# Sending the negated row maxima in two halves, and a new written order of a fused audio tower's attention step

## The chip, the cores and the metric

The kernel runs on one core of one Trainium2 chip. The metric is the device time of one execution in microseconds (us). All times below are of that kind, or are starts and durations of single instructions in one profiled execution, counted from its first instruction.

## The reference

The input is x of 16 sequences (batches) by 256 frames by 128 features. What is computed, cut to what matters:

```python
h = batchnorm(relu(window5(x) @ W.T + b))              # (16, 252, 256)
xn = layernorm(h)
q, k, v = (xn @ Wq, xn @ Wk, xn @ Wv)                  # 16 heads of 16
sim = q @ k.T * 16 ** -0.5 + bias[head, i - j]         # causal: -inf where j > i
h = h + softmax(sim) @ v @ Wo + bo
h = h + ffn(layernorm(h))        # quantised: scales from maxima over the whole tensor
```

## The kernel before, in words

The program has three parts: loading and splitting of weights (to about 64 us), the attention part over 16 batches (to about 496 us), and the feed-forward part, which needs a maximum over all batches and so begins when the last batch is through.

A sequence has N = 252 rows, cut into two tiles of TT = 126. Matrix products run on pairs of f16 values (a high and a low part: `qh`/`ql`, `kh`/`kl`, `xnh`/`xnl`, `onh`/`onl`), accumulated in PSUM. The softmax takes two passes over the scores. Pass P1 puts scores with rows on the partitions into PSUM (line 648 for the bias, line 651 for the product), and VectorE takes the row maxima of each piece (line 803) into `mx`. The maxima of all 16 heads are then turned by TensorE (`mT`, line 659), negated by ScalarE into `mneg` (line 918) and sent by a DMA of the SP queue (line 990) into row 65 of the stacked q tile `q_st`, where the keys' stack holds a row of ones. Pass P2 (line 669) computes the transposed scores with the maximum already subtracted, VectorE adds the bias (line 794, `sbr`), ScalarE takes the exponential (line 879, `pt`), and `PV` multiplies with v (lines 684 and 688). Each pass has 12 pieces a batch: pieces 0 to 5 hold heads 0 to 7, pieces 6 to 11 heads 8 to 15. Each piece uses one of four PSUM banks in turn, and may be written once VectorE has read the piece four places before.

The batches are pipelined through a step b of a loop: P2 and PV of batch b, q, k, v and P1 of batch b+1, the convolution of b+2, the load and transposition of x of b+3, and the second layer norm (`h2`, `stats2`, `xn2`, `x2T`, `x2`) of batch b-1, with the maximum `ax` of batch b-2. Steps -2 to 1 and 12 to 16 are written out, steps 2 to 11 are a loop of two steps a turn. Within a step each engine runs a list written out by hand: `PE_ORDER`, `DVE_ORDER`, `ACT_ORDER` (lines 449 to 462). An entry is a stage and the offset of its batch. An engine runs its list strictly in that order, and each stage waits for the semaphores of its inputs and of the buffers it overwrites.

Stages that need a PSUM bank for a short time share two, listed in `MISC` (lines 496 to 498): bank 6 goes to `q`, `conv`, `xnT` in turn, bank 7 to `mT`, `k`, `x2T`, `v`, `xT`, `OT0`, `onT`. `misc_free` (line 509) makes a stage on TensorE wait until the reader of the stage ahead of it in the ring is done. So before the change `k` waits for `mneg_r`, the sign that `mneg` has read `mT`'s result, and `conv` waits for `ql_r`, the sign that `ql` has read that of `q`.

Around the turn of a step, the orders before are:

```
PE : ... P1[9] P1[10] xnT P1[11] wo | mT q k P2[0..3] conv0 P2[4] conv1 x2T P2[5] conv2 P2[6] PV0 conv3 P2[7] ...
DVE: ... P1[9] onl P1[10] P1[11] xnl | h2 stats2 ql kl ax P2[0] ... P2[11] P1[0] ...
ACT: ... xn onh xnh | mneg qh kh xn2 P2[0..2] x2 P2[3..6] osb0 P2[7..9] relu P2[10] P2[11] osb1 va ...
```

`h2` adds the attention's output to the residual (line 855), `stats2` takes its mean and variance (lines 819, 824), GpSimd turns these into a scale and a shift (lines 952 to 958), ScalarE applies them (`xn2`, line 913), TensorE turns the result (`x2T`, line 726), ScalarE copies it out (`x2`, line 944) and VectorE takes its largest value (`ax`, line 860). `relu` (line 902) begins the chain of the first layer norm over GpSimd (lines 966 to 975), `va` (line 935) copies v out of bank 7. SP's list (`sp_step`, line 985) is: the DMA of `mneg`, six DMAs of q and k into their stacks, the load of x, the store of the residual.

Of the kernel before, what the change touches and what calls it, by code (L numbers as in the profile page):

```python
# [26 lines left out]
ACT = mybir.ActivationFunctionType  # L27
# [5 lines left out]
N = T - CTX + 1  # L33
TT = N // 2
# [37 lines left out]
def audio_tower(nc, x, cw, cb, gamma, beta, rmean, rvar, wq, wk, wv, wo, bo, rel, wg, wu, wd, hot, eyes, out):  # L72
    with ExitStack() as ctx:
# [77 lines left out]
        kS = [sba(f"k_st{i}", [128, H, NP], F16) for i in range(2)]  # L151
        va = [sba(f"va{i}", [128, 2, H, 32]) for i in range(2)]
        qh, ql, kh, kl = (sba(n, [128, 2, NP], F16) for n in ("qh", "ql", "kh", "kl"))
        mneg = sba("mneg", [H, NP], F16)
        qks = sba("qks", [128, 2])
        wam = sba("wam", [128, 8])
        wal = sba("wal", [128, 8])
# [197 lines left out]
        def dve_first(dve):  # L355
            nc.vector.memset(nhalf[:], -0.5).then_inc(S["nhalf_set"], 1)
            nc.vector.memset(epsc[:], EPS).then_inc(S["nhalf_set"], 1)
            nc.vector.memset(minus[:], -1.0).then_inc(S["nhalf_set"], 1)
            nc.vector.memset(lt_s[:, 0:TT - 1], MASKED).then_inc(S["lines_sb"], 1)
            nc.vector.memset(ln_s[:, N:LINE], MASKED).then_inc(S["lines_sb"], 1)  # L360
            for t in kS:
                nc.vector.memset(t[:].rearrange("p h n -> p (h n)").bitcast(F32), TWO_ONES
                                 ).then_inc(S["dve_init"], 1)
            for t in (qh, ql, kh, kl):
                nc.vector.memset(t[:, :, N:NP], 0.0).then_inc(S["dve_init"], 1)
            nc.vector.memset(mneg[:, N:NP], 0.0).then_inc(S["dve_init"], 1)
            dve.wait_ge(S["lines_ps"], 2)
            nc.vector.tensor_copy(lt_s[:, TT - 1:LINE], ps[0:H, 0, TT - 1:LINE]).then_inc(S["lines_sb"], 1)
            nc.vector.tensor_copy(ln_s[:, 0:N], ps[0:H, 1, 0:N]).then_inc(S["lines_sb"], 1)
            dve.wait_ge(S["cw_in"], 16)  # L370
            nc.vector.tensor_reduce(wam[:, 0:1], cw_n.rearrange("p a b -> p (a b)"), X, ALU.max,
                                    apply_absolute_value=True).then_inc(S["wamax"], 1)
            dve_step(dve, -3, 1)
            power(dve, 0, 1, 1, 4, 256)
            dve.wait_ge(S["winv_s"], 1)
            for j in range(len(banks)):
                lo_of(dve, j)
            dve.wait_ge(S["w_loaded"], 64)
# [12 lines left out]
            nc.vector.tensor_tensor(bc[:, 2, :], bc[:, 2, :], shift, ALU.subtract).then_inc(S["vec_ready"], 1)
            dve.wait_ge(S["anti_in"], 16)
            nc.vector.tensor_copy(antib[0:TT], anti[0:TT]).then_inc(S["dve_init"], 1)
            power(dve, 1, 5, 2, 5, 0)
            dve.wait_ge(S["winv_s"], 2)
            nc.vector.tensor_scalar(qks[:, 0:1], wscale[:, W_Q:W_Q + 1], DH ** -0.5, None, ALU.mult
                                    ).then_inc(S["dve_init"], 1)
            nc.vector.tensor_copy(qks[:, 1:2], wscale[:, W_K:W_K + 1]).then_inc(S["dve_init"], 1)
            for t in va:
                nc.vector.memset(t[:, :, :, DH:32], 1.0).then_inc(S["dve_init"], 1)  # L400
            lo_of(dve, len(banks))
            lo_of(dve, len(banks) + 1)
# [46 lines left out]
        PE_ORDER = [("mT", 0, 0), ("q", 1, 0), ("q", 1, 1), ("k", 1, 0), ("k", 1, 1)] + P2[0:4] + [
                    ("conv", 2, 0), P2[4], ("conv", 2, 1), ("x2T", -1, 0), P2[5], ("conv", 2, 2), P2[6], ("PV", 0, 0),  # L450
                    ("conv", 2, 3), P2[7], ("conv", 2, 4), P2[8], ("conv", 2, 5), P2[9], ("PV", 0, 1), P2[10], P2[11],
                    ("v", 1, 0), P1[0], ("v", 1, 1), P1[1], ("PV", 0, 2), P1[2], P1[3], ("xT", 3, 0), P1[4],
                    ("PV", 0, 3), P1[5], P1[6], ("OT0", 0, 0), ("OT1", 0, 0), P1[7], P1[8], ("onT", 0, 0), P1[9],
                    P1[10], ("xnT", 2, 0), P1[11], ("wo", 0, 0), ("wo", 0, 1)]
        DVE_ORDER = [("h2", -1), ("stats2", -1), ("ql", 1), ("kl", 1), ("ax", -2)] + P2 + P1[0:4] + [
                     ("stats", 2), P1[4], ("xl", 3), P1[5], ("on", 0, 0), P1[6], ("on", 0, 1), P1[7], P1[8], P1[9],
                     ("onl", 0), P1[10], P1[11], ("xnl", 2)]
        ACT_ORDER = [("mneg", 0), ("qh", 1), ("kh", 1), ("xn2", -1)] + P2[0:3] + [("x2", -1)] + P2[3:7] + [
                     ("osb", 0, 0)] + P2[7:10] + [("relu", 2)] + P2[10:12] + [
                     ("osb", 0, 1), ("va", 1), ("osb", 0, 2), ("xh", 3), ("osb", 0, 3), ("xn", 2), ("onh", 0),  # L460
                     ("xnh", 2)]


        FF_BANKS = len(ff_banks)
# [17 lines left out]
        def step_order(engine, b):  # L482
# [6 lines left out]
            for st in order:  # L489
                if runs(b, st[1]):  # L490
# [2 lines left out]

        MISC = [[("q", "ql_r", 1, 1, 1), ("conv", "relu_r", 1, 1, 2), ("xnT", "xnl_r", 1, 1, 2)],
                [("mT", "mneg_r", 1, 1, 0), ("k", "kl_r", 1, 1, 1), ("x2T", "x2_r", 1, 1, -1), ("v", "va_r", 1, 1, 1),
                 ("xT", "xl_r", 1, 1, 3), ("OT0", "on_r", 2, 1, 0), ("onT", "onl_r", 1, 1, 0)]]
        misc_at = {m[0]: (r, i) for r, ring in enumerate(MISC) for i, m in enumerate(ring)}
        misc_bank = {name: MB + r for name, (r, i) in misc_at.items()}  # L500
        misc_bank |= {"OT1": OB + 1, "wo": OB}
        PIECES = [st for st in PE_ORDER if st[0] in ("P1", "P2")]
        score_bank = {(kind, n): i % 4 for i, (kind, off, n) in enumerate(PIECES)}

# [47 lines left out]
        def pe_step(pe, b, par):  # L552
            odd = 1 - par
            for st in step_order("pe", b):
# [83 lines left out]
                elif name == "P1":  # L638
# [13 lines left out]
                                                kS[odd][0:P1_ROWS, hd, 0:w], start=False, stop=True,  # L652
                                                skip_group_check=True)
                    last.then_inc(S["p1_ps"], 1)
                elif name == "mT":
                    wait(pe, "mx_r", 12 * (c + 1))
                    misc_free(pe, name, b)
                    for t in range(2):
                        last = nc.tensor.matmul(bank[0:H, t * TT:(t + 1) * TT], mx[0:TT, t, :], identf[0:TT, 0:TT],
                                                start=True, stop=True)  # L660
                    last.then_inc(S["mT_ps"], 1)
                elif name == "P2":
                    if part == 0:
                        wait(pe, "mneg_in", 16 * (c + 1))
                    score_free(pe, st, b)
                    heads, w = piece_heads(part)
                    kt = slice(TT, N) if w == TT else slice(0, TT)
# [99 lines left out]
        def dve_step(dve, b, par):  # L767
            for st in step_order("dve", b):
# [28 lines left out]
                elif name == "P1":  # L797
# [1 line left out]
                    heads, w = piece_heads(n)  # L799
                    wait(dve, "p1_ps", 12 * c + n + 1)  # L800
                    if n == 0:
                        wait(dve, "mT_ps", c)
                    nc.vector.tensor_reduce(mx[0:TT, 0 if w == TT else 1, heads[0]:heads[-1] + 1],  # L803
                                            ps[0:TT, score_bank[name, n], 0:2 * N].rearrange("p (h w) -> p h w", w=w),
                                            X, ALU.max).then_inc(S["mx_r"], 1)
# [58 lines left out]
        def act_step(act, b, par):  # L864
            odd = 1 - par
            for st in step_order("act", b):
# [37 lines left out]
                elif name in ("xn", "xn2"):  # L904
# [7 lines left out]
                    for t in range(2):  # L912
                        nc.scalar.activation(dst[0:TT, t], src[0:TT, t], ACT.Identity, bias=o[0:TT, t:t + 1],
                                             scale=r[0:TT, t:t + 1]).then_inc(S[f"xn{sfx}_r"], 1)
                elif name == "mneg":
                    wait(act, "mT_ps", c + 1)
                    wait(act, "mneg_in", 16 * c)
                    nc.scalar.activation(mneg[:, 0:N], misc("mT")[0:H, 0:N], ACT.Copy, scale=-1.0
                                         ).then_inc(S["mneg_r"], 1)
                elif name == "xnh":  # L920
                    wait(act, "xnT_ps", c + 1)
                    wait(act, "v_ps", c)
# [62 lines left out]
        def sp_step(sp, b, par):  # L985
            odd = 1 - par
            if runs(b, 0):
                unregistered(sp, b)
                wait(sp, "mneg_r", b + 1)
                sp.dma_start(qS[par][P1_ROWS:P2_ROWS], mneg[:]).then_inc(S["mneg_in"], 16)  # L990
            if isinstance(b, int) and b == B - 1:
                wait(sp, "p1_ps", 12 * B)
                wait(sp, "conv_ps", B)
# [17 lines left out]
            if runs(b, -1):  # L1011
# [3 lines left out]
                if isinstance(c, int):  # L1015
                    sp.dma_start(res.ap()[c], hall[0:TT, c, :]).then_inc(S["spilled"], 16)
                else:
                    sp.dma_start(res.ap()[bass.ds(c, 1)].rearrange("a p n -> (a p) n"),
                                 hall[0:TT, bass.ds(c, 1), :].rearrange("p a n -> p (a n)")).then_inc(S["spilled"], 16)

        INIT = 2 + 2 + 4 + 1 + 1 + 2

# [616 lines left out]
```

## Time and profile before

| | |
|---|---|
| median of 3 runs | 791.24 us (788.66 to 792.54) |
| the profiled execution | 793.0 us, of it 791.2 us span from the first to the last instruction |
| busy in the span | PE 620.1, DVE 602.3, ACT 450.2, POOL 162.1 us |
| mean granted TensorE clock | 0.914 of full speed |
| DMA | 52.82 MB |

PE is TensorE, PEld its weight loads, DVE VectorE, ACT ScalarE, POOL GpSimd, SP the queue that issues the DMAs. A duration contains the time in which the result drains, and the next instruction may start before it is over: so twelve matmuls of 0.27 us each follow one another at 0.11 us, and seven instructions of VectorE of 0.67 us take 4.21 us. In a timeline, equal instructions in a row are merged into one line with their count; what stands in square brackets is the idle time just before and what ended it. The clock is 1.00 at 2.4 GHz and 0.50 at 1.2 GHz.

### The profile page before, as it was taken

To read this page: it belongs to the slowest core of one execution; us is meant where nothing else is said; L and a number is where in the kernel's file an instruction comes from. 1 tells how busy PE (TensorE), PEld (TensorE's weight loads), DVE (VectorE), ACT (ScalarE), POOL (GpSimd) and SP (SyncE) were. 2 spreads that over 40 slices of the span, in tenths; PEclk is the share of its full clock that TensorE was granted. 3 is DMA by queue.
4 is the path that set the end of the run, shared out by engine and by line. 5 is a ranking of instruction groups with operands and counts; after the bars stand their busy time and mean duration, and the time that the engine had idled before them with its cause. 6 is when DMAs were issued, how large, how long until landed. Compare 5 with 4: busy or idle time off the path is not lost. (4 is left out here: it accounts for less than half of the span.)

```text
span 791.2 us, 14672 instructions
## 1 busy us (share of the span) xinstructions
PE 620.1 (78%) x5169; PEld 459.6 (58%) x5169; DVE 602.3 (76%) x961; ACT 450.2 (57%) x642; POOL 162.1 (20%) x221
## 2 busy tenths in 40 slices
PE   4579899889989898989899887779999840005998
PEld 2457777777777677767777655334444310005997
DVE  6436877888788878888887787688569998894442
ACT  1436456546654664466456533444389983966872
POOL 4220222132113211221223000000022221760000
PEclk9799999999999999999999895799999985557999
DMA  6334214403440443144213310200024342600533
GB/s 178 124 46 49 36 26 62 62 16 45 60 50 13 57 60 41 19 59 60 34 29 54 55 54 13 80 0 1 1 118 194 121 176 92 215 0 1 155 115 98
DMA packets 39206, 52.82 MB, mean 67 GB/s; under 512 B 5725, under 2 KB 31773, under 8 KB 39165
## 3 DMA queue, kind: packets, MB, share of 16 engines
q1 hardware_dynamic: 38012, 51.49, 29.3%
q10 hardware_dynamic: 1152, 0.79, 0.4%
q8 instruction: 26, 0.43, 0.2%
q14 instruction: 16, 0.12, 0.1%
HBM read 22.74 MB, written 16.81 MB: 50 GB/s over the span
## 5 line engine op out<-in xcount | busy, mean ns | idle before, releaser
L803 DVE TENSOR_REDUCE mx<-ps 126x2 f32<-126x504 f32 (+1 forms) x192 | 125.7, 676 | 32.7 <-PE ps L651 31.4
L794 DVE TENSOR_TENSOR sbr<-ps,biasT 126x504 f32<-126x504 f32 x192 | 120.3, 676 | 26.8 <-PE ps L669 25.3
L879 ACT ACTIVATE pt<-sbr 126x504 f32<-126x504 f32 x192 | 110.8, 618 | 31.2 <-DVE sbr L794 25.0
L669 PE MATMUL ps<-q_st,k_st 66*126 66x252 f16 (+1 forms) x512 | 67.5, 257 | 21.6 <-DVE sbr L794 14.5
L648 PE MATMUL ps<-biasN,antib 126*126 126x504 bf16 x192 | 74.2, 386 | 4.4 <-DMA k_st<-kl 4.4
L651 PE MATMUL ps<-k_st,q_st 65*126 65x252 f16 (+1 forms) x512 | 73.6, 245 | 0.0
L1145 PE MATMUL ps<-x2t,wgT 128*128 128x504 f16 x288 | 66.9, 394 | 8.1 <-ACT gat L1487 4.7
L651 PEld LDWEIGHTS ps<-k_st,q_st 65*126 65x126 f16 x512 | 59.3, 137 | 16.9 <-issue 1.9
L669 PEld LDWEIGHTS ps<-q_st,k_st 66*126 66x126 f16 x512 | 50.2, 142 | 31.9 <-DVE sbr L794 20.1
L1454 PE MATMUL ps<-wdT,raws 128*126 128x256 f16 x480 | 65.1, 278 | 4.5 <-DVE raws L1402 2.8
L1145 PE MATMUL ps<-x2t,wuT 128*128 128x504 f16 x288 | 63.0, 376 | 5.1 <-ACT raws L1501 5.1
L594 PE MATMUL ps<-wcT,xh 128*126 128x256 f16 x320 | 63.2, 280 | 0.1
L1122 PE MATMUL ps<-identf,sc 128*128 128x128 f32 x5 | 2.2, 434 | 75.4 <-DVE sc L1392 51.7
L1454 PEld LDWEIGHTS ps<-wdT,raws 128*126 128x126 f16 x480 | 56.6, 139 | 5.3 <-DVE raws L1402 3.1
L966 POOL TENSOR_TENSOR h<-h,bc 126x512 f32<-126x512 f32 x16 | 20.6, 1287 | 174.0 <-ACT h L902 174.0
L1145 PEld LDWEIGHTS ps<-x2t,wgT 128*128 128x128 f16 x288 | 29.0, 102 | 43.4 <-DVE x2t L1288 8.8
L1567 POOL TENSOR_SCALAR sq<-sig 128x1512 int32<-128x1512 f32 x16 | 23.5, 1467 | 139.4 <-ACT sig L1523 104.9
L1145 PEld LDWEIGHTS ps<-x2t,wuT 128*128 128x128 f16 x288 | 27.4, 98 | 40.3 <-ACT raws L1501 9.6
L952 POOL TENSOR_TENSOR ve<-mv,epsc 126x2 f32<-126x2 f32 x32 | 6.3, 197 | 195.9 <-DVE mv L824 195.9
L1122 PEld LDWEIGHTS ps<-identf,sc 128*128 128x128 f32 x5 | 0.9, 172 | 76.8 <-DVE sc L1392 52.0
L594 PE MATMUL ps<-wcT,xl 128*126 128x256 f16 x160 | 44.5, 278 | 0.0
L684 PE MATMUL ps<-pt,va 126*32 126x252 f32 x512 | 43.1, 410 | 0.8 <-ACT osb L893 0.5
(195 smaller groups left out, 1450.4 us busy)
## 6 DMA issues: line engine op xcount, KB each, us to landing
up_raw<-raws SPq DMA_DIRECT2D x11, 756.0 KB, 3.2
x2t<-up_raw SPq DMA_DIRECT2D x6, 756.0 KB, 6.5
q_st<-qh SPq DMA_DIRECT2D x32, 128.0 KB, 3.7
k_st<-kh SPq DMA_DIRECT2D x32, 128.0 KB, 5.1
res<-hall SPq DMA_DIRECT2D x16, 252.0 KB
x2t<-res SPq DMA_DIRECT2D x16, 252.0 KB
out<-x2t SPq DMA_DIRECT2D x16, 252.0 KB
raws<-up_raw SPq DMA_DIRECT2D x5, 756.0 KB, 4.3
```

The lines of the kernel that those rows point to most:

```text
L594: last = nc.tensor.matmul(bank[0:TT, t * C:(t + 1) * C], *products[i], start=(i == 0), stop=False)
L648: nc.tensor.matmul(dst, antib[0:TT], biasN[0:TT, heads[0]:heads[-1] + 1, N - w:N], start=True, stop=True)
L651: last = nc.tensor.matmul(dst[:, n * w:(n + 1) * w], qS[odd][0:P1_ROWS, hd, qt], kS[odd][0:P1_ROWS, hd, 0:w], start=False, stop=True, skip ...
L669: last = nc.tensor.matmul(ps[0:TT, score_bank[name, part], n * w:(n + 1) * w], kS[par][0:P2_ROWS, hd, kt], qS[par][0:P2_ROWS, hd, N - w:N] ...
L684: nc.tensor.matmul(ps[32 * i:32 * i + 32, OB + g % 2, 0:N], vc[0:TT, 0, 4 * g + i, :], p[:, i // 2, (i % 2) * N:(i % 2) * N + N], start=Tr ...
L794: nc.vector.tensor_tensor(sbr[0:TT, n % 4].rearrange("p (h w) -> p h w", w=w), ps[0:TT, score_bank[name, n], 0:2 * N].rearrange("p (h w) - ...
L803: nc.vector.tensor_reduce(mx[0:TT, 0 if w == TT else 1, heads[0]:heads[-1] + 1], ps[0:TT, score_bank[name, n], 0:2 * N].rearrange("p (h w) ...
L879: nc.scalar.activation(pt[0:TT, n // 3 % 2, n % 3], sbr[0:TT, n % 4], ACT.Exp).then_inc(S["exp_r"], 1)
L966: nc.gpsimd.tensor_tensor(h[0:TT], h[0:TT], bc[0:TT, 1:2, :].broadcast_to([TT, 2, C]), ALU.mult).then_inc(S["v1_r"], 1)
L1145: last = nc.tensor.matmul(ps[:, 3 * half + j, 0:2 * N], w[:, wp, k, m], xq[:, at:at + 2 * N], start=(i == 0), stop=(i == 5))
L1454: last = nc.tensor.matmul(down_at(c, bb, t), o[c % 2][:, m, rows], wdT[:, w, m], start=(m == 0 and i == 0), stop=(m == MT - 1 and i == 2))
L1567: nc.gpsimd.tensor_scalar(sq[t % 2][:], sig[t % 2][:], 65536.0, 0.0, ALU.mult, ALU.add).then_inc(S["sq_r"], 1)
```

## The change

The maxima are turned, negated and sent in two halves: half A (heads 0 to 7) of the next batch late in a step, when pieces 0 to 5 of P1 have been reduced, half B (heads 8 to 15) at the start of the next step. P2[0] waits for half A alone, P2[6] for half B. The orders are rewritten. `OT0` leaves the ring of bank 7 for bank 4; `mTA` joins that ring, `mTB` the ring of bank 6 ahead of `q`. Of the two DMAs at the end of the diff, that of half B stands first in SP's list of a step, and that of half A last.

```diff
-        mneg = sba("mneg", [H, NP], F16)
+        mneg = sba("mneg", [H // 2, 2, NP], F16)
...
+        PE_ORDER = [P2[0], P2[1], ("mTB", 0, 0), ("q", 1, 0), ("q", 1, 1), P2[2], ("k", 1, 0), ("k", 1, 1), P2[3],
+                    ("conv", 2, 0), P2[4], ("conv", 2, 1), P2[5], ("conv", 2, 2), P2[6], ("PV", 0, 0), P2[7],
+                    ("x2T", -1, 0), ("conv", 2, 3), P2[8], ("conv", 2, 4), P2[9], ("conv", 2, 5), P2[10],
+                    ("PV", 0, 1), P2[11], ("v", 1, 0), P1[0], ("v", 1, 1), P1[1], ("xT", 3, 0), P1[2],
+                    ("PV", 0, 2), P1[3], P1[4], ("PV", 0, 3), P1[5], P1[6], ("OT0", 0, 0), ("OT1", 0, 0), P1[7],
+                    ("mTA", 1, 0), P1[8], ("onT", 0, 0), P1[9], P1[10], ("xnT", 2, 0), P1[11], ("wo", 0, 0),
+                    ("wo", 0, 1)]
+        DVE_ORDER = [P2[0], ("h2", -1), P2[1], ("ql", 1), ("stats2", -1), P2[2], ("kl", 1), P2[3], P2[4], ("ax", -2)
+                     ] + P2[5:12] + P1[0:3] + [("stats", 2), P1[3], ("xl", 3), P1[4], P1[5], ("on", 0, 0), P1[6],
+                     ("on", 0, 1), P1[7], P1[8], P1[9], ("onl", 0), P1[10], P1[11], ("xnl", 2)]
+        ACT_ORDER = [("mnegB", 0), P2[0], ("qh", 1), P2[1], ("kh", 1), P2[2], P2[3], P2[4], P2[5], ("xn2", -1),
+                     P2[6], ("osb", 0, 0), P2[7], P2[8], ("x2", -1), P2[9], ("relu", 2), P2[10], P2[11],
+                     ("osb", 0, 1), ("va", 1), ("xh", 3), ("osb", 0, 2), ("osb", 0, 3), ("xn", 2), ("mnegA", 1),
+                     ("onh", 0), ("xnh", 2)]
...
-        MISC = [[("q", "ql_r", 1, 1, 1), ("conv", "relu_r", 1, 1, 2), ("xnT", "xnl_r", 1, 1, 2)],
-                [("mT", "mneg_r", 1, 1, 0), ("k", "kl_r", 1, 1, 1), ("x2T", "x2_r", 1, 1, -1), ("v", "va_r", 1, 1, 1),
-                 ("xT", "xl_r", 1, 1, 3), ("OT0", "on_r", 2, 1, 0), ("onT", "onl_r", 1, 1, 0)]]
+        MISC = [[("mTB", "mneg_r", 2, 2, 0), ("q", "ql_r", 1, 1, 1), ("conv", "relu_r", 1, 1, 2),
+                 ("xnT", "xnl_r", 1, 1, 2)],
+                [("k", "kl_r", 1, 1, 1), ("x2T", "x2_r", 1, 1, -1), ("v", "va_r", 1, 1, 1), ("xT", "xl_r", 1, 1, 3),
+                 ("mTA", "mneg_r", 2, 1, 1), ("onT", "onl_r", 1, 1, 0)]]
...
+                elif name in ("mTA", "mTB"):
+                    half = "AB".index(name[2])
+                    wait(pe, "mx_r", 12 * c + 6 * (half + 1))
+                    misc_free(pe, name, b)
                     for t in range(2):
+                        last = nc.tensor.matmul(bank[0:H // 2, t * TT:(t + 1) * TT],
+                                                mx[0:TT, t, half * H // 2:(half + 1) * H // 2], identf[0:TT, 0:TT],
+                                                start=True, stop=True)
...
                 elif name == "P2":
                     if part == 0:
-                        wait(pe, "mneg_in", 16 * (c + 1))
+                        wait(pe, "mneg_in", 32 * c + 16)
+                    elif part == 6:
+                        wait(pe, "mneg_in", 32 * c + 32)
...
+                elif name in ("mnegA", "mnegB"):
+                    half = "AB".index(name[4])
+                    wait(act, "mT_ps", 2 * c + half + 1)
+                    wait(act, "mneg_in", 32 * c + 16 * half - 16)
+                    nc.scalar.activation(mneg[:, half, 0:N], misc("mT" + name[4])[0:H // 2, 0:N], ACT.Copy,
+                                         scale=-1.0).then_inc(S["mneg_r"], 1)
...
+                sp.dma_start(qS[par][P1_ROWS:P2_ROWS, H // 2:H], mneg[:, 1]).then_inc(S["mneg_in"], 16)
...
+                sp.dma_start(qS[odd][P1_ROWS:P2_ROWS, 0:H // 2], mneg[:, 0]).then_inc(S["mneg_in"], 16)
```

## Rows read from the trace of the kernel before

**Rows 1.** Windows (steady step, step 1): us; busy of PE, PEld, DVE, ACT, POOL; clock; DMA.
```profile
280.29:307.10 26.81, 24.12 (x248) 19.66 (x247) 22.47 (x44) 15.00 (x29) 6.16 (x11) 1.00 0.33 44
90.60:119.40 28.80, 25.83 (x248) 21.37 (x247) 21.94 (x43) 15.15 (x29) 6.16 (x11) 0.94 0.31 43
```
**Rows 2.** Timeline of ACT, two steps running: start, us, engine, line, operation, idle before.
```profile
280.29 0.37 ACT L918 ACTIVATE mneg<-ps 16x252 f16<-16x252 f32 x1 [2.11 <-PE ps L659]
307.10 0.37 ACT L918 ACTIVATE mneg<-ps 16x252 f16<-16x252 f32 x1 [2.11 <-PE ps L659]
```
**Rows 3.** Timeline of PE at the start of that step: mT, q, P2, conv, P2[4].
```profile
279.57 0.60 PE L659 MATMUL ps<-identf,mx 126*16 126x126 f32 x4
280.10 0.39 PE L623 MATMUL ps<-xnh,wqT 128*128 128x252 f16 x2
...
282.72 1.04 PE L669 MATMUL ps<-q_st,k_st 66*126 66x252 f16 x10
283.60 0.27 PE L594 MATMUL ps<-wcT,xh 128*126 128x256 f16 x1
...
285.61 0.43 PE L669 MATMUL ps<-q_st,k_st 66*126 66x252 f16 x2 [1.30 <-DVE sbr L794]
```
**Rows 4.** Timeline of DVE there: h2, end of stats2, ql, kl, ax, P2.
```profile
279.81 0.75 DVE L855 SCALAR_TENSOR_TENSOR hall<-ps,wscale,hall 126x512 f32 x1
...
281.33 0.37 DVE L824 BATCH_NORM_AGGREGATE mv<-bns 126x2 f32<-126x6 f32 x2
282.52 0.74 DVE L834 SCALAR_TENSOR_TENSOR ql<-ps,qks,qh 128x504 f16<-128x504 f32 x1 [0.82 <-ACT qh L930]
283.63 0.74 DVE L834 SCALAR_TENSOR_TENSOR kl<-ps,qks,kh 128x504 f16<-128x504 f32 x1 [0.38 <-ACT kh L930]
284.29 0.67 DVE L860 TENSOR_REDUCE amax_x<-x2t  x1
284.88 4.21 DVE L794 TENSOR_TENSOR sbr<-ps,biasT 126x504 f32<-126x504 f32 x7
```
**Rows 5.** Timeline of ACT there: qh, xn2, exponentials; and va.
```profile
281.70 0.68 ACT L930 ACTIVATE qh<-ps,qks 128x504 f16<-128x504 f32 x1 [1.04 <-PE ps L623]
...
283.50 1.08 ACT L913 ACTIVATE xn<-hall,nb,rstd 126x256 f32 x2
285.67 1.71 ACT L879 ACTIVATE pt<-sbr 126x504 f32<-126x504 f32 x3 [1.09 <-DVE sbr L794]
...
294.73 0.68 ACT L935 ACTIVATE va<-ps,wscale 126x512 f32<-126x512 f32 x1
```
**Rows 6.** Timeline of PE further on: x2T, conv3, PV1, v, P1[2], onT.
```profile
286.42 0.59 PE L726 MATMUL ps<-identf,xn 126*128 126x126 f32 x4
...
288.83 0.32 PE L594 MATMUL ps<-wcT,xh 128*126 128x256 f16 x1
...
291.38 0.63 PE L684 MATMUL ps<-pt,va 126*32 126x252 f32 x8
...
292.66 0.27 PE L548 MATMUL ps<-wvT,xnh 128*126 128x256 f16 x1
...
295.70 0.43 PE L648 MATMUL ps<-biasN,antib 126*126 126x504 bf16 x1
...
302.43 0.65 PE L705 MATMUL ps<-identf,on 126*128 126x126 f32 x4 [0.79 <-DVE on L844]
```
**Rows 7.** Page, DMA issues: KB each, median us to landing.
```profile
k_st<-kl SPq DMA_DIRECT2D x16, 128.0 KB, 5.6
...
q_st<-mneg SPq DMA_DIRECT2D x16, 8.0 KB, 1.9
```
**Rows 8.** Timeline of PE: P2[0] and conv3 of step 1, P2[0] of step 15.
```profile
95.03 1.33 PE L669 MATMUL ps<-q_st,k_st 66*126 66x252 f16 x10 [1.76 <-DMA q_st<-mneg]
...
101.33 0.32 PE L594 MATMUL ps<-wcT,xh 128*126 128x256 f16 x1
...
468.99 1.09 PE L669 MATMUL ps<-q_st,k_st 66*126 66x252 f16 x10 [2.30 <-DMA q_st<-mneg]
```

More of the change, by code:

```diff
@@ L365, in dve_first @@
                 nc.vector.memset(t[:, :, N:NP], 0.0).then_inc(S["dve_init"], 1)
-            nc.vector.memset(mneg[:, N:NP], 0.0).then_inc(S["dve_init"], 1)
+            nc.vector.memset(mneg[:, :, N:NP], 0.0).then_inc(S["dve_init"], 1)
             dve.wait_ge(S["lines_ps"], 2)
@@ L448, in audio_tower @@
         P2, P1 = pieces("P2", 0, 0, 12), pieces("P1", 1, 0, 12)
[L449 to L461, printed above, removed]
+        PE_ORDER = [P2[0], P2[1], ("mTB", 0, 0), ("q", 1, 0), ("q", 1, 1), P2[2], ("k", 1, 0), ("k", 1, 1), P2[3],
[5 more added lines that the diff above has]
+                    ("wo", 0, 1)]
@@ L492, in step_order @@
             return todo
-        MISC = [[("q", "ql_r", 1, 1, 1), ("conv", "relu_r", 1, 1, 2), ("xnT", "xnl_r", 1, 1, 2)],
-                [("mT", "mneg_r", 1, 1, 0), ("k", "kl_r", 1, 1, 1), ("x2T", "x2_r", 1, 1, -1), ("v", "va_r", 1, 1, 1),
-                 ("xT", "xl_r", 1, 1, 3), ("OT0", "on_r", 2, 1, 0), ("onT", "onl_r", 1, 1, 0)]]
+        MISC = [[("mTB", "mneg_r", 2, 2, 0), ("q", "ql_r", 1, 1, 1), ("conv", "relu_r", 1, 1, 2),
+                 ("xnT", "xnl_r", 1, 1, 2)],
+                [("k", "kl_r", 1, 1, 1), ("x2T", "x2_r", 1, 1, -1), ("v", "va_r", 1, 1, 1), ("xT", "xl_r", 1, 1, 3),
+                 ("mTA", "mneg_r", 2, 1, 1), ("onT", "onl_r", 1, 1, 0)]]
         misc_at = {m[0]: (r, i) for r, ring in enumerate(MISC) for i, m in enumerate(ring)}
         misc_bank = {name: MB + r for name, (r, i) in misc_at.items()}
-        misc_bank |= {"OT1": OB + 1, "wo": OB}
+        misc_bank |= {"OT0": OB, "OT1": OB + 1, "wo": OB}
         PIECES = [st for st in PE_ORDER if st[0] in ("P1", "P2")]
@@ L654, in pe_step @@
                     last.then_inc(S["p1_ps"], 1)
-                elif name == "mT":
-                    wait(pe, "mx_r", 12 * (c + 1))
+                elif name in ("mTA", "mTB"):
+                    half = "AB".index(name[2])
+                    wait(pe, "mx_r", 12 * c + 6 * (half + 1))
                     misc_free(pe, name, b)
                     for t in range(2):
-                        last = nc.tensor.matmul(bank[0:H, t * TT:(t + 1) * TT], mx[0:TT, t, :], identf[0:TT, 0:TT],
+                        last = nc.tensor.matmul(bank[0:H // 2, t * TT:(t + 1) * TT],
+                                                mx[0:TT, t, half * H // 2:(half + 1) * H // 2], identf[0:TT, 0:TT],
                                                 start=True, stop=True)
@@ L801, in dve_step @@
                     if n == 0:
-                        wait(dve, "mT_ps", c)
+                        wait(dve, "mT_ps", 2 * c)
                     nc.vector.tensor_reduce(mx[0:TT, 0 if w == TT else 1, heads[0]:heads[-1] + 1],
@@ L914, in act_step @@
                                              scale=r[0:TT, t:t + 1]).then_inc(S[f"xn{sfx}_r"], 1)
[L915 to L919, printed above, removed]
+                elif name in ("mnegA", "mnegB"):
[4 more added lines that the diff above has]
+                                         scale=-1.0).then_inc(S["mneg_r"], 1)
                 elif name == "xnh":
@@ L988, in sp_step @@
                 unregistered(sp, b)
-                wait(sp, "mneg_r", b + 1)
-                sp.dma_start(qS[par][P1_ROWS:P2_ROWS], mneg[:]).then_inc(S["mneg_in"], 16)
+                sent, ready = valued(sp, 32 * b + 16), valued(sp, 2 * b + 2)
+                wait(sp, "mneg_in", sent)
+                wait(sp, "mneg_r", ready)
+                sp.dma_start(qS[par][P1_ROWS:P2_ROWS, H // 2:H], mneg[:, 1]).then_inc(S["mneg_in"], 16)
             if isinstance(b, int) and b == B - 1:
@@ L1019, in sp_step @@
                                  hall[0:TT, bass.ds(c, 1), :].rearrange("p a n -> p (a n)")).then_inc(S["spilled"], 16)
+            if runs(b, 1):
+                unregistered(sp, b)
+                sent, ready = valued(sp, 32 * (b + 1)), valued(sp, 2 * b + 3)
+                wait(sp, "mneg_in", sent)
+                wait(sp, "mneg_r", ready)
+                sp.dma_start(qS[odd][P1_ROWS:P2_ROWS, 0:H // 2], mneg[:, 0]).then_inc(S["mneg_in"], 16)
         INIT = 2 + 2 + 4 + 1 + 1 + 2
```

## The prediction, made before the change was run

> **What bounds the kernel now.** I read the windows first, then the timelines of one steady step, engine by engine, and last the places at which TensorE stood longest. Most steps of the attention part take 26.81 us from one negation of maxima to the next [rows 2]. In such a step no engine is full: the records of TensorE cover 24.1 us and those of VectorE 22.5 [rows 1], and TensorE's overlap one another, so it is less full than it looks. What sets the period is an alternation: each engine goes strictly through its written list, and one waits for the other a little at many places. The wait at which the change aims is at the start. Measure from t = 0 at 279.48, when the product with Wo has been issued. `mT` starts at 0.09, `q` at 0.62, P2[0] on TensorE at 3.24 [rows 3]. VectorE does `h2`, `stats2`, `ql`, `kl` and `ax` first and comes to P2[0] at 5.40 [rows 4]. TensorE gets through P2[0..3] and a part of the convolution and stands 1.30 us for a bank, until P2[4] at 6.13 [rows 3]. About 22 of VectorE's 26.8 us are work in either kernel, so the order alone can give or take a few us a step.
>
> **The change, part by part.** I walk the new lists from the same t = 0, with the durations of the rows and the time from an operation's start to the start of its follower as the rows show it.
>
> *The extra half.* `mT` becomes two stages of two matmuls each, with 8 columns of maxima instead of 16; no row shows that shape. It is bounded by nothing and by all of the present `mT`, 0.53 us of TensorE until `q` starts [rows 3]. The streamed side stays as wide, so I take 0.53. It lies inside the 0.79 us for which `onT` waits for VectorE [rows 6]; without that wait it would cost 14 x 0.5 = 7 us. The second negation, 0.37 on ScalarE, stands where ScalarE waits 2.11 us today [rows 2]. The second DMA goes last in SP's list, where nothing is queued behind it but the next step, and half B goes ahead of the stack DMAs as `mneg` did. Half A is negated by about t = 25.4 and lands 1.9 us later [rows 7], some 2 us before P2[0] wants it. So P2[0] does begin right behind `wo`.
>
> *The first wait.* TensorE does P2[0], P2[1] (0.22 each: four pieces from 282.72 to 283.60 [rows 3]) and starts `mTB` at 0.58. The negation starts 0.72 after it, as now (279.57 to 280.29 [rows 2, 3]), and ends at 1.67. Before, that time was covered: `mT` was in `k`'s ring. Now the next user of its bank is `q`, directly behind it, so `q` starts at 1.73 instead of 0.62 and everything behind it on TensorE stands 0.6. `qh` starts 1.60 after `q` [rows 3, 5], at 3.33, and `ql` 0.82 later [rows 4, 5], at 4.15. VectorE is through P2[0], `h2` and P2[1] at 2.34 (0.60 to 0.70 each by the spacing of [rows 4]). `stats2` could run but stands behind `ql`: VectorE idles 1.8 us where it idled 0.82 [rows 4].
>
> *The second wait, the dear one.* From 4.15 VectorE does `ql` 0.66, `stats2` 1.0, P2[2] 0.6, `kl` 0.66, P2[3] and P2[4] 1.2, `ax` 0.59 [rows 4]. P2[5] starts at 8.85 and ends at 9.52. ScalarE has P2[5] in its list **ahead of** `xn2`: the exponential runs to 10.26 and `xn2`, 1.08 us [rows 5], to about 11.25. (The scale from GpSimd is there 1.8 after the end of `stats2`, 281.70 to 283.50 [rows 4, 5], by 7.7: no matter.) `x2T` can start at 11.31. Before, `xn2` stood ahead of all exponentials and `x2T` ran at 6.94 [rows 6]. TensorE meanwhile: `k` to 4.57, P2[3], conv0 from 4.94 (held by `ql`) to 5.50, P2[4], conv1 (0.55), P2[5], conv2 (0.65), P2[6] at 7.15, PV0 to 8.23, P2[7] to 8.46. So P2[4] comes 0.6 earlier than now, but `x2T` is next in TensorE's list and holds it for 2.85 us. Queued behind it are conv3 and P2[8], hence VectorE too, which is through P2[7] at 10.6 and stands 2.2. conv3 starts at 11.80, against 9.35 now [rows 6]. From conv3 to `v` took 3.83 us [rows 6]; P2[7] is out of that stretch, so 3.6, and `v` starts at 15.40 against 13.18: **+2.2 us**.
>
> *The third wait.* `xT` moves from behind P1[3] to behind P1[1] and must wait for `va`, the reader of `v` in the same bank. PV1 starts at 14.37 and is done at 15.3; only then may ScalarE write the exponentials of P2[9] (its buffer is the one that PV1 reads), then `relu`, P2[10], P2[11], about 0.55 each [rows 5], `osb1`, 0.3, and `va`, 0.68 [rows 5], to 18.48. TensorE is there at 17.58 and stands 0.95. P1[2] starts at 18.76 against 16.22 [rows 6]: **+2.5**. That `OT0` no longer waits for `xl` saves nothing, as TensorE comes there late. The remaining pieces alternate as now, with about 0.1 more. The stack DMAs leave up to 2.3 us later (`kl` at 6.4 against 4.15 [rows 4]), land 5.6 after the issue [rows 7], before P1[0] at 16.0. **A full step takes 29.4 us, +2.6.**
>
> *The steps at the ends.* Steps 1 to 14 have all of it: 14 x 2.6 = 36.4. Steps -1 and 0 have no `x2T`: +0.5 for `mTA` and `va` together. In step 15 there is no q, k or convolution: P2[0] is free of its DMA, which held TensorE 2.30 us [rows 8], a gain of about 3, of which the wait for `x2T` gives back 1.7: -1.3.
>
> *The clock.* In step 1 TensorE stood 1.76 us and came back at half rate: from P2[0] to conv3 took 6.30 us [rows 8] against 6.11 with a wait of 1.30 within [rows 3, 6], that is 4.81 of work, so a slow stretch at 1.2 GHz costs 1.5; the mean clock of that step is 0.94, that of the steady one 1.00 [rows 1]. The new wait of 2.85 is longer than that one and than the 1.30 that leaves the clock at 2.4 GHz. The bounds are 0 and 14 x 1.5 = 21 us. As part of a slow stretch will lie in waits, I take half: 10.5.
>
> The Trainium skill (TensorE: Matmul & The Clock Gate, HAM oscillation) gives a rule of thumb for idle gaps by which one as short as this would leave the clock up. By that rule the sum would be 10.5 less; the row of step 1 speaks against it.
>
> The sum is 36.4 + 0.5 - 1.3 + 10.5 = +46 on the profiled execution's 793.0 (791.2 span and 1.8 around it): 839. The median of the runs is 791.24, so 1.8 less: about 838.
>
> **The rivals.**
> (a) *The wait for `x2T` is short.* If `q` is not held by `mTB`'s reader, or VectorE's idle 1.8 is not there, P2[5] ends near 7.7, `x2T` starts at 9.5 and holds TensorE 1 us, too short for the clock. A step gains 0.6 and loses some 1.4: +0.8, 14 x 0.8 = 11, so 802. For it: all the late terms hang on that one delay. Against: the order of the lists is fixed, and negation after transposition is in the rows.
> (b) *Faster: the early second pass pays.* Its place is TensorE's P2[4], 0.6 earlier. If nothing is late behind it, 14 x 0.6 + 1.3 is -9.7, so 782. It decides by the end of `xn2`: only if that lies before 8.5 (I have 11.25) is TensorE not held. VectorE's work ahead of it alone reaches 7.7 to P2[5]'s end, and exponential and `xn2` take 1.7 more, so it needs shorter operations than the rows show.
> (c) *No difference:* gain and waits cancel, as would be so with a step between those of (a) and (b): 791.
> (d) *The change doesn't do what it says:* half A is held on its way through ScalarE or SP by more than the 2 us spare, and P2[0] waits for it besides the rest; at 1 us a step, 852.
>
> **How the numbers follow.** My forecast 0.70 (of it 0.25 with hardly any clock term, near 828, as the steady loop's waits leave the clock up), (a) 0.12, (b) 0.09, (c) 0.05, (d) 0.04. A difference of 0.5%, 4 us, is about what a measurement of this kernel can tell from none. Slower by over that are the forecast, (a) and (d), 0.86; faster (b), 0.09; the same (c), 0.05. The range: without the clock term 828, with all of it 848; each of the three waits of the walk is uncertain by 0.3 to 0.5 us a step, some 8 us in all, to 857 above. Below it reaches into (a), to 804, and leaves out (b), (c) and the rest of (a).
>
> **What would show it.** In the profile after: negations of half B 29 to 30.5 us apart; `q` about 1.1 after `mTB`; `ql` preceded by 1.5 to 2 us of idle VectorE; the transposition `x2T` preceded by 2 to 3 us of idle TensorE released by ScalarE's `xn2`; `xT` preceded by up to 1 us released by `va`; a mean clock of some steps under 1.00. Wrong, if `x2T` is not waited for by more than 1 us, or if P2[0] waits for its DMA.

## The result, and the profile of the changed kernel

The changed kernel takes 839.59 us (median of 4 runs, 837.73 to 842.58), the kernel before 790.94 us beside it: a ratio of 1.0615 with a 95% interval of 1.0587 to 1.0643. Forecast were 838 and slower. The profiled execution took 840.07 us, its span 838.2, against 791.2 before: 47.0 us more.

First the page, with the busy times of the engines, the granted clock in 40 slices, and two groups of instructions (busy us, mean ns, idle time before them and what ended it):

```profile
PE 647.7 (77%) x5233; PEld 480.3 (57%) x5233; DVE 600.9 (72%) x961; ACT 456.3 (54%) x658; POOL 162.0 (19%) x221
...
PEclk9799999999999999999999988789999995555999
...
L800 DVE TENSOR_TENSOR sbr<-ps,biasT 126x504 f32<-126x504 f32 x192 | 125.4, 677 | 65.6 <-PE ps L675 64.7
...
L675 PE MATMUL ps<-q_st,k_st 66*126 66x252 f16 (+1 forms) x512 | 79.3, 269 | 3.4 <-DVE sbr L800 2.5
```

The last row is what the change wanted: TensorE waits 3.4 us in all ahead of the pieces of P2, where it waited 21.6. The row above is what it got instead: VectorE's waits for those pieces rise from 26.8 to 65.6 us.

Next the windows: a steady step, step 1 and step 2 (us; busy us and count of PE, PEld, DVE, ACT, POOL; clock, DMA share, GB/s).

```profile
272.82:303.50 30.68, 26.69 (x250) 21.68 (x250) 22.46 (x45) 15.45 (x30) 6.16 (x11) 0.94 0.28 39
91.20:119.43 28.23, 24.92 (x250) 20.04 (x250) 21.60 (x43) 15.40 (x30) 6.17 (x11) 1.00 0.32 44
119.43:150.11 30.68, 26.70 (x250) 21.69 (x250) 22.37 (x44) 15.46 (x31) 6.16 (x11) 0.94 0.29 41
```

A steady step takes 30.68 us instead of 26.81 [rows 1, 2], and the clock's mean in it is 0.94 instead of 1.00. Step 1 is the exception, with 28.23 us at the full clock; it has no `ax` yet, and TensorE waits 1.69 us for `x2T` there. The kernel before had its only slow stretch of the early steps in step 1, where P2[0] waited for its DMA [rows 1, 8]; half A is there in time, so this one is gone. Now TensorE in that steady step, the first of the three windows (start, us, engine, line; idle time just before, and what ended it). Its zero, the end of `wo`, is 271.61.

```profile
272.19 0.60 PE L662 MATMUL ps<-identf,mx 126*8 126x126 f32 x4
273.25 0.39 PE L625 MATMUL ps<-xnh,wqT 128*128 128x252 f16 x2 [0.46 <-ACT mneg L925]
...
282.66 0.65 PE L732 MATMUL ps<-identf,xn 126*128 126x126 f32 x4 [2.38 <-ACT xn L919]
283.14 0.38 PE L596 MATMUL ps<-wcT,xh 128*126 128x256 f16 x1
283.31 0.42 PE L596 MATMUL ps<-wcT,xl 128*126 128x256 f16 x1
...
288.36 0.27 PE L550 MATMUL ps<-wvT,xnh 128*126 128x256 f16 x1
...
291.43 0.30 PE L580 MATMUL ps<-identf,xin 128*128 128x128 f32 x1 [0.73 <-ACT va L942]
```

The three waits stand where the prediction put them: `q` for the negation, 0.46; `x2T` for `xn2`, 2.38; `xT` for `va`, 0.73. Behind the long one the same matmul takes 0.42 us instead of 0.27: the clock has gone to half. Three windows show it, in the wait, behind it and after the stretch:

```profile
279.00:282.60 3.60, 1.27 (x20) 0.61 (x18) 3.14 (x6) 2.81 (x6) 0.00 (x0) 1.00 1.17 116
283.20:286.50 3.30, 3.30 (x19) 3.30 (x18) 0.86 (x2) 1.64 (x4) 0.00 (x0) 0.50 0.51 101
287.00:288.00 1.00, 1.00 (x20) 0.55 (x18) 0.60 (x2) 0.00 (x0) 0.00 (x0) 1.00 0.00 0
```

TensorE is busy through the whole of the slow one. From conv3 (283.14) to `v` (288.36) it is 5.22 us, in step 1 at full clock 3.56 (100.73 to 104.29). VectorE and ScalarE show how `xn2` comes to be late:

```profile
275.65 0.74 DVE L840 SCALAR_TENSOR_TENSOR ql<-ps,qks,qh 128x504 f16<-128x504 f32 x1 [1.55 <-ACT qh L937]
...
280.30 1.85 DVE L800 TENSOR_TENSOR sbr<-ps,biasT 126x504 f32<-126x504 f32 x3
284.84 0.68 DVE L800 TENSOR_TENSOR sbr<-ps,biasT 126x504 f32<-126x504 f32 x1 [2.70 <-PE ps L675]
```

```profile
281.00 0.62 ACT L885 ACTIVATE pt<-sbr 126x504 f32<-126x504 f32 x1 [0.55 <-DVE sbr L800]
281.53 1.07 ACT L919 ACTIVATE xn<-hall,nb,rstd 126x256 f32 x2
```

VectorE waits 1.55 us for `qh`, and P2[5] starts at 280.30; its exponential and then `xn2` follow, and `x2T` is released at 282.66. VectorE, having done P2[5..7], then stands 2.70 us itself. The chain closes in a ring: late VectorE, late ScalarE, late TensorE, idle VectorE.

Where did the 47.0 us go? From the first negation of half B (65.39) to the one of step 15 (514.37) it is 448.98 us, against 401.88 (64.84 to 466.72) before: +47.1. What lies before adds 0.55, and what follows takes 323.8 us instead of 324.5. Step 0 takes 25.81 against 25.75 and step 1 28.23 against 28.85, so the loss is wholly in steps 2 to 14: 3.87 us in each of steps 2 to 10, and 2.1 in step 14.

### The profile page after: what moved, and what is told of

The parts are those of the page before. It is cut to its first block and busy times, and to the rows that moved or that the text cites. A ratio compares the mean times of both kernels' runs of the same rounds, so it can differ in the third digit from the quotient of the medians.

```text
span 838.2 us, 14909 instructions
## 1 busy us (share of the span) xinstructions
PE 647.7 (77%) x5233; PEld 480.3 (57%) x5233; DVE 600.9 (72%) x961; ACT 456.3 (54%) x658; POOL 162.0 (19%) x221
## 5 line engine op out<-in xcount | busy, mean ns | idle before, releaser
L800 DVE TENSOR_TENSOR sbr<-ps,biasT 126x504 f32<-126x504 f32 x192 | 125.4, 677 | 65.6 <-PE ps L675 64.7
L885 ACT ACTIVATE pt<-sbr 126x504 f32<-126x504 f32 x192 | 116.1, 617 | 76.8 <-DVE sbr L800 54.1
L675 PE MATMUL ps<-q_st,k_st 66*126 66x252 f16 (+1 forms) x512 | 79.3, 269 | 3.4 <-DVE sbr L800 2.5
L596 PE MATMUL ps<-wcT,xh 128*126 128x256 f16 x320 | 74.5, 317 | 0.7
L675 PEld LDWEIGHTS ps<-q_st,k_st 66*126 66x126 f16 x512 | 59.0, 153 | 11.2 <-issue 4.9
L596 PE MATMUL ps<-wcT,xl 128*126 128x256 f16 x160 | 50.6, 317 | 0.0
L596 PEld LDWEIGHTS ps<-wcT,xh 128*126 128x126 f16 x320 | 48.3, 164 | 3.4 <-issue 3.0
L925 ACT ACTIVATE mneg<-ps 8x252 f16<-8x252 f32 x32 | 11.8, 370 | 61.4 <-PE ps L662 61.4
```

The source lines that it names most:

```text
L596: last = nc.tensor.matmul(bank[0:TT, t * C:(t + 1) * C], *products[i], start=(i == 0), stop=False)
L675: last = nc.tensor.matmul(ps[0:TT, score_bank[name, part], n * w:(n + 1) * w], kS[par][0:P2_ROWS, hd, kt], qS[par][0:P2_ROWS, hd, N - w:N] ...
L800: nc.vector.tensor_tensor(sbr[0:TT, n % 4].rearrange("p (h w) -> p h w", w=w), ps[0:TT, score_bank[name, n], 0:2 * N].rearrange("p (h w) - ...
L885: nc.scalar.activation(pt[0:TT, n // 3 % 2, n % 3], sbr[0:TT, n % 4], ACT.Exp).then_inc(S["exp_r"], 1)
```

## The experiments

All ratios are to the kernel before, timed on the same chip. A "step" is the distance of two neighbouring negations of half B (of the whole, in the kernel before) in the steady part, the mean of two steps unless one is named.

| run | us (median) | ratio, 95% interval | step, us |
|---|---|---|---|
| xn2 early | 781.79 | 0.9874 (0.9841 to 0.9907) | 26.43 |
| wait filled | 817.92 | 1.0330 (1.0306 to 1.0355) | 29.04 |
| halves only | 784.96 | 0.9901 (0.9868 to 0.9935) | 26.49 |
| stats2 first | 814.48 | 1.0300 (1.0271 to 1.0329) | 28.14 |
| xT back | 824.61 | 1.0411 (1.0382 to 1.0439) | 30.09 or 28.43 |
| OT0 alone | 785.57 | 0.9908 (0.9890 to 0.9926) | 26.42 |
| xn2 and stats2 | 780.86 | 0.9853 (0.9830 to 0.9877) | 26.40 |
| all four | 774.63 | 0.9758 (0.9730 to 0.9786) | 25.80 |

**One entry moved in ScalarE's list.** From the changed kernel:

```diff
-                     ("kh", 1), P2[2], P2[3], P2[4], P2[5], ("xn2", -1),
+                     ("kh", 1), P2[2], ("xn2", -1), P2[3], P2[4], P2[5],
```

> The changed kernel with xn2 moved ahead in ScalarE's list, from behind P2[5] to behind P2[2]; nothing else. Theory: x2T is held by xn2 alone, and that wait also drops the clock. Then xn2 ends about 8.6 after the end of wo, x2T is waited for by 0.2 to 0.5 us instead of 2.4, the clock of the steady steps goes back to 1.00, and a step falls from 30.7 us to about 26.5 to 27: some 14 x 4 = 55 us less, 780 to 795. Rival (the other new waits, of q for mTB's reader, of ql and of xT for va, carry the loss): the time falls by less than 20 us and stays over 815.

Measured: 781.79, within the theory's 780 to 795 and 58 us under the changed kernel. The windows of two steps running:

```profile
275.17:301.61 26.44, 24.95 (x250) 20.08 (x250) 22.09 (x44) 15.26 (x31) 6.17 (x11) 1.00 0.33 45
301.61:328.04 26.43, 24.88 (x250) 20.11 (x250) 22.18 (x45) 15.28 (x30) 6.17 (x11) 1.00 0.33 45
```

and the same stage on ScalarE and on TensorE:

```profile
280.42 0.62 ACT L885 ACTIVATE pt<-sbr 126x504 f32<-126x504 f32 x1 [1.09 <-DVE sbr L800]
281.35 1.09 ACT L919 ACTIVATE xn<-hall,nb,rstd 126x256 f32 x2 [0.30 <-POOL nb L965]
```

```profile
282.49 0.65 PE L732 MATMUL ps<-identf,xn 126*128 126x126 f32 x4
```

`xn2` now waits for GpSimd's scale, the earliest it can, and `x2T` has no idle time ahead of it. The clock is back at 1.00 and the step at 26.43, 4.25 us shorter. The other new waits are all still there (`q`'s 0.54 or 0.46, VectorE's 1.63 or 1.55 before `ql`, `xT`'s 0.69), so the rival, that these carry the loss, falls. One entry in one list turns a kernel that is 6.2% slower into one that is 1.3% faster than before. Most of this 1.3% will turn out to be another edit's: see "What gained 6 us".

**What of it is the clock.** In the changed kernel, TensorE is given work for the time of its wait:

```diff
                 elif name == "x2T":
-                    wait(pe, "xn2_r", 2 * (c + 1))
                     misc_free(pe, name, b)
+                    for _ in range(16):
+                        nc.tensor.matmul(bank[0:TT, 0:C], ones[:], cbx[:], start=True, stop=True)
+                    wait(pe, "xn2_r", 2 * (c + 1))
```

> The changed kernel with 16 matmuls (256 columns, 0.11 us each, 1.8 us in all) issued into x2T's own bank ahead of its wait for xn2; x2T overwrites them. The wait stays as long, only TensorE works in it. Theory (a slow stretch of the clock adds 1.5 to 2 us to each steady step): the steady steps' clock is 1.00, a step takes 28.7 to 29, the total is 815 to 822. Rival (the clock costs nothing, since the engines wait anyway, or TensorE's own work is delayed by the filling): 835 to 842.

Measured: 817.92, within the theory's 815 to 822. TensorE around the wait, and the window of a step:

```profile
302.74 1.91 PE L730 MATMUL ps<-cbx,ones 128*126 128x256 bf16 x16
305.36 0.65 PE L734 MATMUL ps<-identf,xn 126*128 126x126 f32 x4 [0.71 <-ACT xn L921]
```

```profile
295.45:324.48 29.03, 26.79 (x266) 21.78 (x266) 22.36 (x44) 15.46 (x31) 6.16 (x11) 1.00 0.30 41
```

The same chain still releases `x2T`, only 0.71 us of the wait are left idle, and the steady clock stays at 1.00. A step falls from 30.68 to 29.04: the half clock is worth **1.64 us a step**, 22 us of the whole. Useless work made the kernel faster. So the 3.87 us by which a step grew split into 1.64 of clock and 2.23 of waits.

**The halves alone.** The list of the kernel before, with `mTB` and `mnegB` in the place of `mT` and `mneg`, `mTA` behind P1[7], `mnegA` behind `xn`, and `OT0` in bank 4 as in the changed kernel:

```diff
-        PE_ORDER = [("mT", 0, 0), ("q", 1, 0), ("q", 1, 1), ("k", 1, 0), ("k", 1, 1)] + P2[0:4] + [
+        PE_ORDER = [("mTB", 0, 0), ("q", 1, 0), ("q", 1, 1), ("k", 1, 0), ("k", 1, 1)] + P2[0:4] + [
...
-                    ("PV", 0, 3), P1[5], P1[6], ("OT0", 0, 0), ("OT1", 0, 0), P1[7], P1[8], ("onT", 0, 0), P1[9],
+                    ("PV", 0, 3), P1[5], P1[6], ("OT0", 0, 0), ("OT1", 0, 0), P1[7], ("mTA", 1, 0), P1[8], ("onT", 0, 0), P1[9],
...
-                [("mT", "mneg_r", 1, 1, 0), ("k", "kl_r", 1, 1, 1), ("x2T", "x2_r", 1, 1, -1), ("v", "va_r", 1, 1, 1),
-                 ("xT", "xl_r", 1, 1, 3), ("OT0", "on_r", 2, 1, 0), ("onT", "onl_r", 1, 1, 0)]]
+                [("mTB", "mneg_r", 2, 2, 0), ("k", "kl_r", 1, 1, 1), ("x2T", "x2_r", 1, 1, -1), ("v", "va_r", 1, 1, 1),
+                 ("xT", "xl_r", 1, 1, 3), ("mTA", "mneg_r", 2, 1, 1), ("onT", "onl_r", 1, 1, 0)]]
```

> The halves alone: two transpositions, two negations, two DMAs, in the order of the kernel before (mTB where mT was, in the ring ahead of k; mTA behind P1[7], its negation behind xn; P2[0] where it was). Theory (the halves cost little, mTA lies in onT's wait): 788 to 795. Rival (0.5 us of TensorE a step is on the path): 797 to 800.

Measured: 784.96, faster than either theory allowed. The halves cost nothing that shows, and something in this kernel gains 6 us. The run with `OT0` alone, further down, looks for it.

**VectorE's idle time.** In the changed kernel:

```diff
-        DVE_ORDER = [P2[0], ("h2", -1), P2[1], ("ql", 1), ("stats2", -1), P2[2], ("kl", 1), P2[3], P2[4], ("ax", -2)
+        DVE_ORDER = [P2[0], ("h2", -1), P2[1], ("stats2", -1), ("ql", 1), P2[2], ("kl", 1), P2[3], P2[4], ("ax", -2)
```

> The changed kernel with stats2 ahead of ql in VectorE's list, so that VectorE works while it waits for q. Theory (x2T is late through VectorE's delay too): VectorE's wait before ql falls from 1.55 to 0.5 us, P2[5] and xn2 come 1 us earlier, x2T's wait is 1.4 instead of 2.4. A step is 1 us shorter if the clock still drops (826) and up to 2.8 shorter if it doesn't (800). Rival: no gain, 837 to 842, if ql and the stacks behind it are what matters.

Measured: 814.48, between the theory's two ends. VectorE's wait for `qh` falls to 0.70 us, `x2T`'s to 1.52:

```profile
296.62 0.65 PE L732 MATMUL ps<-identf,xn 126*128 126x126 f32 x4 [1.52 <-ACT xn L919]
```

```profile
259.46:287.64 28.18, 25.05 (x250) 20.03 (x250) 22.52 (x45) 15.44 (x30) 6.15 (x11) 1.00 0.31 42
```

A step takes 28.14, at the full clock here; of steps 2 to 12 three (9, 11 and 12) show 0.94 and take 1.6 to 1.7 more, as the one from 315.74:

```profile
315.74:345.56 29.82, 26.69 (x250) 21.68 (x250) 22.50 (x45) 15.44 (x30) 6.15 (x11) 0.94 0.29 40
```

Its wait for `x2T` is 1.53, like that of the fast steps beside it. Against the filled wait (29.04) the 0.86 us less of waiting is 0.90 us less of step: the wait for `x2T` is on the path, near enough one for one.

**The third wait.** In the changed kernel, `xT` back to its place of before:

```diff
-                    ("PV", 0, 1), P2[11], ("v", 1, 0), P1[0], ("v", 1, 1), P1[1], ("xT", 3, 0), P1[2],
-                    ("PV", 0, 2), P1[3], P1[4], ("PV", 0, 3), P1[5], P1[6], ("OT0", 0, 0), ("OT1", 0, 0), P1[7],
+                    ("PV", 0, 1), P2[11], ("v", 1, 0), P1[0], ("v", 1, 1), P1[1], ("PV", 0, 2), P1[2],
+                    P1[3], ("xT", 3, 0), P1[4], ("PV", 0, 3), P1[5], P1[6], ("OT0", 0, 0), ("OT1", 0, 0), P1[7],
```

(with `xh` and `xl` moved likewise, and `stats` behind P1[3]).

> The changed kernel with xT back behind P1[3] (and xh, xl, stats where they stood before); the rest as changed. Theory (the third wait, 0.7 us of TensorE for va, is a loss of its own): a step is 0.5 to 0.7 us shorter, 830 to 833. Rival (TensorE's 0.7 us there is lost anyway, because VectorE or the clock's slow stretch sets the pace): within 3 us of the changed kernel, 837 to 842.

Measured: 824.61, a larger gain than either theory allowed. The wait ahead of `xT` is gone. Two neighbouring steps of this run tell the rest:

```profile
236.89:265.32 28.43, 24.85 (x250) 19.95 (x250) 22.18 (x44) 15.45 (x31) 6.14 (x11) 1.00 0.31 42
265.32:295.40 30.08, 26.50 (x250) 21.61 (x250) 22.27 (x45) 15.44 (x30) 6.14 (x11) 0.94 0.29 39
```

Both have the long wait for `x2T`:

```profile
246.80 0.65 PE L732 MATMUL ps<-identf,xn 126*128 126x126 f32 x4 [2.45 <-ACT xn L919]
...
275.15 0.65 PE L732 MATMUL ps<-identf,xn 126*128 126x126 f32 x4 [2.38 <-ACT xn L919]
```

The first keeps the full clock all the same, the second does not, and they are 1.65 us apart: the price of one slow stretch, a second time and within one kernel. A slow step is 0.60 us shorter than the changed kernel's (30.08 against 30.68), a fast one 0.61 shorter than with the filled wait (28.43 against 29.04). So moving `xT` is worth 0.6 us a step, some 8 us, and the other 7 come from steps that no longer drop the clock: in this trace 3, 6, 9, 12 and 13.

**What gained 6 us.** The kernel before, with `OT0` in bank 4:

```diff
-                 ("xT", "xl_r", 1, 1, 3), ("OT0", "on_r", 2, 1, 0), ("onT", "onl_r", 1, 1, 0)]]
+                 ("xT", "xl_r", 1, 1, 3), ("onT", "onl_r", 1, 1, 0)]]
...
-        misc_bank |= {"OT1": OB + 1, "wo": OB}
+        misc_bank |= {"OT0": OB, "OT1": OB + 1, "wo": OB}
```

> The kernel before with OT0 in bank 4 instead of in the ring of bank 7, nothing else. Theory (the 6 us that the halves alone gained come from OT0 no longer waiting for xl, 0.46 us of TensorE a step, and the halves themselves cost next to nothing): 783 to 787. Rival (they come from P2[0] no longer waiting for the maxima): 789 to 793.

Measured: 785.57, within the theory's 783 to 787; a step of 26.42, like the halves only (784.96, 26.49). The gain is the bank: before, TensorE waited 5.6 us in all (13 times) for `xl` ahead of `OT0`, and here never. The halves by themselves are worth nothing either way, within their intervals. And the step is 26.42 here and 26.43 with `xn2` early: with the dear wait gone, but those for the negation and for `va` still there, the second pass begun early has won nothing over this one edit of a bank.

**What is left when `x2T` isn't held.** Both moves in the changed kernel:

```diff
-        DVE_ORDER = [P2[0], ("h2", -1), P2[1], ("ql", 1), ("stats2", -1), P2[2], ("kl", 1), P2[3], P2[4], ("ax", -2)
+        DVE_ORDER = [P2[0], ("h2", -1), P2[1], ("stats2", -1), ("ql", 1), P2[2], ("kl", 1), P2[3], P2[4], ("ax", -2)
...
-                     ("kh", 1), P2[2], P2[3], P2[4], P2[5], ("xn2", -1),
+                     ("kh", 1), P2[2], ("xn2", -1), P2[3], P2[4], P2[5],
```

> The changed kernel with both xn2 behind P2[2] and stats2 ahead of ql. If VectorE's 1.55 us of waiting for ql still counts once x2T isn't held: a step of 25.5 to 26, 766 to 775. If TensorE's list is then the bound: 26.2 to 26.4 a step, 778 to 782.

Measured: 780.86, against 781.79 with `xn2` alone: no difference. The second reading holds: VectorE's 1.55 us before `ql` cost next to nothing by themselves. They were dear only through the `xn2` behind them.

**All four mended.** As above, with `xT` back too, and

```diff
-        PE_ORDER = [P2[0], P2[1], ("mTB", 0, 0), ("q", 1, 0), ("q", 1, 1), P2[2], ("k", 1, 0), ("k", 1, 1), P2[3],
+        PE_ORDER = [P2[0], P2[1], ("mTB", 0, 0), P2[2], ("q", 1, 0), ("q", 1, 1), ("k", 1, 0), ("k", 1, 1), P2[3],
```

> The changed kernel with all four orders mended: xn2 behind P2[2], stats2 ahead of ql, xT back behind P1[3], and P2[2] between mTB and q to cover the negation. If each of TensorE's waits is on the path, a step loses 0.7 (va) and 0.2 (q) more than in the kernel with only xn2 and stats2 moved: 765 to 772. If not, it is equal to that one.

Measured: 774.63, the ratio 0.9758. It beats both kernels, but falls between the two forecasts, 765 to 772 and no gain over 780.86. Two steps of it:

```profile
245.60:271.44 25.84, 24.86 (x253) 20.12 (x254) 22.25 (x45) 15.37 (x30) 6.15 (x11) 1.00 0.34 46
271.44:297.20 25.76, 24.69 (x251) 19.95 (x250) 22.08 (x44) 15.37 (x30) 6.14 (x11) 1.00 0.34 46
```

A step is 0.60 shorter than with `xn2` and `stats2` moved, which is what `xT` was worth above; so the P2[2] that covers the negation has added little or nothing. The trace shows why: in the second of these steps `q` waits 0.17 us instead of the 0.54 of the run before, but being later it makes the first convolution behind it wait 0.31 for `ql`, where there was no wait. The changed order is thus worth something when its lists fit: 785.57 to 774.63, from 26.42 to 25.80 us a step. Which of its parts gives the 0.62 was not taken apart.

## Why the prediction was right, and where it only seemed so

**The total** came out at 839.6 against 838, and the mechanism was the one walked. But two terms were off by about 10 us each, in opposite directions, and hid each other: that the total hit within 2 us was luck, as the sizes go.

- **The waits** were put at +2.6 us a full step, 14 x 2.6 = 36.4, and 35.6 with the ends. With the clock held up the whole grows by 26.5 (817.92 against 791.42 beside it). Two things were off. A steady step grows by 2.23 (29.04 against 26.81), for the walk was a little late at each link: `q` at 1.73 against 1.64 (273.25 less 271.61), P2[5] at 8.85 against 8.69, `x2T` at 11.31 against 11.05. And not all of 14 steps have it. With the wait filled, step 1 takes 28.24 against 28.85 before: it had a wait for the DMA and a slow stretch to lose (clock 0.94 [rows 1]), which the prediction used for its price and did not take off the sum. Steps 13 and 14 grow by 1.53 and -0.35; step 14 before had a clock of 0.87.
- **The clock** was put at half of the bounds, 0.75 us a step and 10.5 in all. It is 1.64 a step, 22 in all (839.59 against 817.92). The price of one slow stretch, 1.5 from [rows 8], was near to the 1.64 and 1.65 measured. Wrong was the halving: in the changed kernel every steady step from step 2 on has such a stretch, and hardly any of it lies in waits, for in the step shown the stretch begins about 0.5 us after TensorE comes back to work, and in the 3.30 us of it that are shown TensorE is busy for 3.30.
- **The first wait**, of `q`: there, 0.46 against 0.6. **VectorE's idle time** before `ql`: there, 1.55 against 1.8. That it matters only through `x2T` is shown by the pair of runs with `stats2` first: 25 us with `xn2` late (0.90 a step of shorter wait, the rest from steps that keep the clock), 1 us with `xn2` early.
- **The second wait**, the dear one: there, 2.38 against 2.85, released by `xn2`, and its removal alone gives back 58 us, more than the whole loss.
- **The third wait**: there, 0.73. The walk added 0.3 for it, from +2.2 to +2.5; the run with `xT` back shows 0.6 a step. Here the walk was short.
- **The extra half**: 0.53 of TensorE, taken as hidden in `onT`'s wait [rows 6]. Shown by the halves only: no loss against `OT0` alone, and `onT`'s wait in the steady step falls from 1.03 to 0.45, about the price of the half. The narrower transposition takes the same 0.27 us a matmul as the wide one, so taking the whole price was right.
- **`OT0`'s bank** "saves nothing": so in the changed order perhaps, but in the order before it saves 0.4 us a step and 7 us in all. The prediction did not ask what this edit is worth by itself.
- **Step 15** was put at -1.3; from its negation to the end it was -0.7. Steps -1 and 0 were put at +0.5 and took +0.55 and +0.06.
- **The rivals.** (a), a short wait for `x2T`, is what `stats2` first makes: 814, not 802, since 1.52 us of wait were left where it assumed 1 (some 7 us), and three steps and more dropped the clock all the same (some 5). (b), faster, decides by the end of `xn2`, it said, from 8.5 on: with `xn2` early the matmul of `x2T` isn't waited for, and the kernel is 58 us faster than as changed, at 782. That this is (b)'s number is chance: (b) had no gain from the bank of `OT0` in it and no wait for `va`. Its argument against, that operations would have to be shorter, held for the order as given. (c), no difference, is 49 us away. (d) did not occur: P2[0] waits for no DMA in the steady steps.

In the changed kernel the clock fell in every steady step, with a wait of 2.38 or 2.45 us in it; with `xT` back in two of three steps with such a wait; with `stats2` first in 3 of 11 with one of 1.5 to 1.7. The Trainium skill's rule of thumb (TensorE: Matmul & The Clock Gate, HAM oscillation), by which gaps as short as these leave the clock up, is not borne out by that.

## What to carry to other kernels

Where each engine runs a list written by hand, a stage moved later on one engine is paid for by whoever waits for it: look for the consumer's place in the other engine's list, and put the producer directly where its inputs are ready. Idle time on one engine says nothing of its worth until one knows which stage is behind it; here the same 1.55 us were worth 25 us or 1. A wait of TensorE can cost more than its length, since the clock may halve behind it, so price it with a slow stretch from the trace. A step paid it whole or not at all, 1.64 or 0 here; half of it, as an average, hides that the two cases are 22 us apart.

## What the runs showed of the hardware that was not expected

A wait of the same length did not always have the same effect. With `xT` back, one step in three of the loop kept the full clock (28.43 us), with a wait of 2.45 us in one and 2.39 in another, and the two behind it lost it (30.08 each). In the changed kernel, all the steady steps lose it with 2.38 or 2.45. With `stats2` first the wait is 1.52 and most steps keep it. So the length of the wait alone does not decide; what does was not tried further. And keeping TensorE busy with products that nobody reads was worth 22 us.
